# Both layer norms' normalisation moved from VectorE to ScalarE, and a small copy written as a reduction

## What is computed

```python
x = x + attn(layernorm(x))      # 16 heads of 8, causal softmax, w_qkv, w_proj, biases
x = x + ffn(layernorm(x))
# layernorm(x) = (x - mean(x)) / sqrt(var(x) + 1e-5), over the 128 channels, no gain or bias
# ffn: probs = sigmoid(x @ Wg + bg); weights = probs * (probs > 0.5)
#      sum over 8 experts e of weights[:, e] * (relu(x @ W1[e] + b1[e]) @ W2[e] + b2[e]), hidden 512
```

## Time and profile before

| | before |
|---|---|
| median of three runs | 685.77 us (685.29 to 686.74) |
| profiled execution: its own time | 686.17 us |
| its span, first to last instruction | 684.4 us |
| TensorE matmul busy | 650.2 us (95%) |
| VectorE, ScalarE, GpSimd busy | 480.8, 418.6, 330.9 us |
| mean granted TensorE clock | 0.989 of full speed |

### The profile page before, as it was taken

How to read it: one execution, slowest core, us unless ns; L and a number is a source line. 1 busy time by engine, 2 the same in 40 slices (tenths; PEclk the granted TensorE clock), 3 DMA queues, 4 the chain that set the end, 5 groups by cost and what they waited for, 6 DMA issues and landing times.

```text
span 684.4 us, 13158 instructions
## 1 busy us (share of the span) xinstructions
PE 650.2 (95%) x4486; PEld 449.4 (66%) x4486; DVE 480.8 (70%) x958; ACT 418.6 (61%) x793; POOL 330.9 (48%) x409
## 2 busy tenths in 40 slices
PE   2799999999999989999999989999999999999996
PEld 2355666667666766667666756667666766677774
DVE  5797687679876796669866696668866676546443
ACT  2158656667666666676666566666666666665553
POOL 4018434556435454556335555455245564545554
PEclk9799999999999999999999999999999999999998
DMA  6442213210322113210222113220222102100310
GB/s 191 111 125 52 51 42 104 57 42 17 87 73 57 41 26 108 69 42 18 86 63 54 40 39 106 57 56 3 59 87 57 42 2 80 48 17 6 103 32 16
DMA packets 29954, 40.44 MB, mean 59 GB/s; under 512 B 4064, under 2 KB 14184, under 8 KB 29888
## 3 DMA queue, kind: packets, MB, share of 16 engines
q1 hardware_dynamic: 29360, 39.40, 21.4%
q10 hardware_dynamic: 528, 0.20, 0.1%
HBM read 23.72 MB, written 2.23 MB: 38 GB/s over the span
## 4 chain that ended last, share of the span: by engine, by line
PE 85%; DVE 6%; issue 3%; DMA 2%; SPq 2%; POOL 1%; ACT 1%; POOLq 0%; DVEq 0%
PE ring L1166 11%; PE ring L1248 10%; PE ring L1107 9%; PE ring L1109 9%; PE ring L1108 9%; PE y_bank L1293 8%; PE y_bank L1297 8%; PE y_bank L1295 8%; PE ring L1178 6%; PE ring L1113 3%; DVE xn L910 2%; PE ring L1193 2%; DVE negmax L1018 1%; DMA g_w<-in_L_ffn_b 1%; PE ring L1228 1%
## 5 line engine op out<-in xcount | busy, mean ns | idle before, releaser
L863 ACT ACTIVATE h_hi<-ring 128x512 fp32r<-128x512 f32 x256 | 153.4, 599 | 126.2 <-PE ring L1109 110.2
L831 ACT ACTIVATE pt<-ring 128x512 f32<-128x512 f32 x313 | 172.0, 596 | 54.7 <-PE ring L1166 51.8
L762 POOL TENSOR_TENSOR h_lo<-h_all,h_hi 128x512 fp32r<-128x512 f32 x96 | 123.9, 1290 | 149.5 <-ACT h_all L869 149.0
L1018 DVE TENSOR_REDUCE negmax<-ring 128x1 f32<-128x512 f32 (+1 forms) x185 | 119.2, 683 | 74.3 <-PE ring L1178 74.2
L1070 DVE SCALAR_TENSOR_TENSOR h_lo<-ring,h_hi 128x512 fp32r<-128x512 f32 x160 | 109.5, 686 | 56.0 <-ACT h_hi L863 52.7
L755 POOL TENSOR_SCALAR_AFFINE_SELECT pt<-pt 128x512 f32<-128x512 f32 x128 | 80.1, 640 | 110.9 <-ACT pt L831 110.8
L1293 PE MATMUL y_bank<-h_hi,w_lo 128*128 128x512 f32 x256 | 109.0, 426 | 1.1 <-DVE f_buf L1083 0.5
L1107 PE MATMUL ring<-x2T_lo,w_hi 128*128 128x512 f32 x256 | 108.0, 422 | 0.3 <-DVE negmax L1018 0.3
L1166 PE MATMUL ring<-stack 32*128 32x256 f32 (+3 forms) x992 | 94.9, 363 | 8.7 <-DMA stack<-stack 4.8
L1297 PE MATMUL y_bank<-h_lo,w_hi 128*128 128x512 f32 x256 | 100.6, 393 | 0.0
L1109 PE MATMUL ring<-x2T_hi,w_hi 128*128 128x512 f32 x256 | 100.5, 393 | 0.0
(11 more groups left out here) (119 smaller groups left out, 754.1 us busy)
## 6 DMA issues: line engine op xcount, KB each, us to landing
f_buf<-gates SPq DMA_DIRECT2D x64, 256.0 KB, 3.3
stack<-parts SPq DMA_DIRECT2D x96, 128.0 KB
x_in<-in_L_attn_x SPq DMA_DIRECT2D x8, 256.0 KB, 2.9
f_buf<-in_L_ffn_W SPq DMA_DIRECT2D x1, 2048.0 KB, 10.4
out_x<-f_buf SPq DMA_DIRECT2D x8, 256.0 KB, 2.3
stack<-nmT SPq DMA_DIRECT2D x64, 8.0 KB
stack<-stack SPq DMA_DIRECT2D x32, 16.0 KB
bv<-in_L_attn_b_qkv SPq DMA_DIRECT2D x1, 256.0 KB
```

Of the source, the lines that this page charges most:

```text
L762: g_.tensor_tensor(h_lo[:, (i * SLOTS + s) % 3, :], h_all[:], h_hi[:, (i * SLOTS + s) % 3, :].bitcast(F32), ALU.subtract).then_inc(s_hlo_p ...
L831: sc.activation(pt[:, slot, :], b[:], ACT.Exp, scale=SCALE).then_inc(free_sem("ex", i, g, u), 1)
L863: sc.activation(h_hi[:, (i * SLOTS + s) % 3, :], bank_of("z", i, s)[:], ACT.Relu).then_inc(s_hhi, 1)
L1018: v.tensor_reduce(dst, src, AX.X, ALU.max, negate=True).then_inc(free_sem("max", i, g, u), 1)
```

## The change

In `work_items` the items ln1n and ln2n go from VectorE to ScalarE (booked at 1130 instead of 1110 ns), rs1 and rs2 are booked at 1620 instead of 1300, and the waits that follow from it are added. Since the order of all engines comes out of `list_schedule`, it is computed anew. GpSimd now also computes shift = -mean * rstd, and ScalarE computes xn = rstd * x + shift by an activation with a per-partition scale and bias. In `merge` the copy becomes a minimum over one element.

```diff
-         ('dve', 'ln2n', False): 8.5,
+         ('act', 'ln2n', False): 8.5,
...
-            put("sp", ("xload", i), t0 - 30, 600, ("dve", ("ln1n", i - 2)), ("pool", ("xbp", i - 2)))
+            put("sp", ("xload", i), t0 - 30, 600, ("act", ("ln1n", i - 2)), ("pool", ("xbp", i - 2)))
...
-        put("dve", ("ln1b", i), t0 - 20.9, 350, ("dve", ("ln1a", i)))
-        put("pool", ("rs1", i), t0 - 20.8, 1300, ("dve", ("ln1b", i)), ("pool", ("ident", None)))
-        put("dve", ("ln1n", i), t0 - 19, 1110, ("pool", ("rs1", i)), ("pe", ("xT", i - 1)),
+        put("dve", ("ln1b", i), t0 - 20.9, 350, ("dve", ("ln1a", i)), ("pool", ("rs1", i - 1)))
+        put("pool", ("rs1", i), t0 - 20.8, 1620, ("dve", ("ln1b", i)), ("act", ("ln1n", i - 1)), ("pool", ("ident", None)))
+        put("act", ("ln1n", i), t0 - 19, 1130, ("pool", ("rs1", i)), ("pe", ("xT", i - 1)),
             ("pe", ("x2T", i - 3)))
-        put("pe", ("xT", i), t0 - 17, 450, ("dve", ("ln1n", i)), ("pe", ("v", i - 1)))
+        put("pe", ("xT", i), t0 - 17, 450, ("act", ("ln1n", i)), ("pe", ("v", i - 1)))
...
         put("dve", ("proj", i), at + 1.8, 700, ("pe", ("proj", i)), ("pool", ("xbp", i)),
-            ("dve", ("yT", i - 2)))
+            ("dve", ("yT", i - 2)), ("act", ("ln2n", i - 2)))
         put("dve", ("ln2a", i), at + 1.9, 860, ("dve", ("proj", i)))
-        put("dve", ("ln2b", i), at + 1.9, 350, ("dve", ("ln2a", i)))
-        put("pool", ("rs2", i), at + 1.9, 1300, ("dve", ("ln2b", i)))
-        put("dve", ("ln2n", i), at + 2, 1110, ("pool", ("rs2", i)),
+        put("dve", ("ln2b", i), at + 1.9, 350, ("dve", ("ln2a", i)), ("pool", ("rs2", i - 1)))
+        put("pool", ("rs2", i), at + 1.9, 1620, ("dve", ("ln2b", i)), ("act", ("ln2n", i - 1)))
+        put("act", ("ln2n", i), at + 2, 1130, ("pool", ("rs2", i)),
             ("pe", ("xT", min(i + 2, BATCH - 1))), ("pe", ("x2T", i - 1)))
...
                 elif kind in ("rs1", "rs2"):
                     n = int(kind == "rs2")
                     pool.wait_ge(s_aggr[n], (i + 1) * TB)
+                    if i:
+                        pool.wait_ge(s_x2n if n else s_xn, i * TB)
                     g_.tensor_scalar(var[:, n], mv[:, n, :, 1], EPS, None,
                                      ALU.add).then_inc(s_var[n], 1)
-                    pool.wait_ge(s_var[n], i + 1)
-                    g_.tensor_tensor(rstd[:, n], var[:, n], mhalf[:], ALU.pow).then_inc(s_rs[n], 1)
+                    g_.tensor_scalar(shift[:, n], mv[:, n, :, 0], -1.0, None,
+                                     ALU.mult).then_inc(s_var[n], 1)
+                    pool.wait_ge(s_var[n], 3 * i + 2)
+                    g_.tensor_tensor(rstd[:, n], var[:, n], mhalf[:], ALU.pow).then_inc(s_var[n], 1)
+                    pool.wait_ge(s_var[n], 3 * i + 3)
+                    g_.tensor_tensor(shift[:, n], shift[:, n], rstd[:, n],
+                                     ALU.mult).then_inc(s_rs[n], 1)
...
+            def normalise(n, i, src, dst, done):
+                act.wait_ge(s_rs[n], i + 1)
+                for t in range(TB):
+                    sc.activation(dst[:, t, :], src[:, t, :], ACT.Identity,
+                                  bias=shift[:, n, t:t + 1],
+                                  scale=rstd[:, n, t:t + 1]).then_inc(done, 1)
...
+                elif kind == "ln2n":
+                    act.wait_ge(*full("xT", min(i + 2, BATCH - 1)))
+                    if i:
+                        act.wait_ge(*full("x2T", i - 1))
+                    normalise(1, i, x1[:, i % 2], x2n, s_x2n)
...
                     dve.wait_ge(s_stats[n], (i + 1) * TB)
+                    wait(dve, s_rs[n], i)
...
-                else:
-                    dve.wait_ge(s_rs[n], i + 1)
-                    done = s_x2n if n else s_xn
-                    for t in range(TB):
-                        v.tensor_scalar(dst[:, t, :], src[:, t, :], mv[:, n, t, 0:1],
-                                        rstd[:, n, t:t + 1], ALU.subtract,
-                                        ALU.mult).then_inc(done, 1)
...
-                    v.tensor_copy(negmax[:, g, 0], pm[:, :, :, 3]).then_inc(s_merge, 1)
+                    v.tensor_reduce(negmax[:, g, 0], pm[:, :, :, 3:4], AX.X,
+                                    ALU.min).then_inc(s_merge, 1)
...
                     dve.wait_ge(s_xbp, i + 1)
+                    if i >= 2:
+                        dve.wait_ge(s_x2n, (i - 1) * TB)
```

More of the change, by code:

```diff
@@ L174, in work_items @@
         put("dve", ("v", i), t0 + 12.1, 700, ("pe", ("v", i)), ("dve", ("vset", None)))
-        put("pool", ("xbp", i), t0 + 22, 1280, ("dve", ("ln1n", i)), ("dve", ("proj", i - 1)))
+        put("pool", ("xbp", i), t0 + 22, 1280, ("act", ("ln1n", i)), ("dve", ("proj", i - 1)))
         for g in range(GROUPS):
@@ L212, in work_items @@
         put("dve", ("proj", i), at + 1.8, 700, ("pe", ("proj", i)), ("pool", ("xbp", i)),
-            ("dve", ("yT", i - 2)))
+            ("dve", ("yT", i - 2)), ("act", ("ln2n", i - 2)))
         put("dve", ("ln2a", i), at + 1.9, 860, ("dve", ("proj", i)))
-        put("dve", ("ln2b", i), at + 1.9, 350, ("dve", ("ln2a", i)))
-        put("pool", ("rs2", i), at + 1.9, 1300, ("dve", ("ln2b", i)))
-        put("dve", ("ln2n", i), at + 2, 1110, ("pool", ("rs2", i)),
+        put("dve", ("ln2b", i), at + 1.9, 350, ("dve", ("ln2a", i)), ("pool", ("rs2", i - 1)))
+        put("pool", ("rs2", i), at + 1.9, 1620, ("dve", ("ln2b", i)), ("act", ("ln2n", i - 1)))
+        put("act", ("ln2n", i), at + 2, 1130, ("pool", ("rs2", i)),
             ("pe", ("xT", min(i + 2, BATCH - 1))), ("pe", ("x2T", i - 1)))
-        put("pe", ("x2T", i), at + 2.1, 450, ("dve", ("ln2n", i)))
+        put("pe", ("x2T", i), at + 2.1, 450, ("act", ("ln2n", i)))
         put("act", ("x2T", i), at + 2.2, 600, ("pe", ("x2T", i)), ("pe", ("z", i - 2, SLOTS - 1)))
@@ L483, in block_program @@
         rstd = sb("rstd", [P, 2, TB])
+        shift = sb("shift", [P, 2, TB])
         xT = sb("xT", [P, T])
@@ L793, in _ @@
                                   ACT.Copy).then_inc(s_w2hi, 1)
+                elif kind == "ln1n":
+                    if i:
+                        act.wait_ge(*full("xT", i - 1))
+                    if i >= 3:
+                        act.wait_ge(*full("x2T", i - 3))
+                    normalise(0, i, x_in[:, i % 2], xn, s_xn)
+                elif kind == "ln2n":
+                    act.wait_ge(*full("xT", min(i + 2, BATCH - 1)))
+                    if i:
+                        act.wait_ge(*full("x2T", i - 1))
+                    normalise(1, i, x1[:, i % 2], x2n, s_x2n)
                 elif kind == "xT":
@@ L896, in prepare_small_weights, with statistics @@
                 v.memset(wg_lo[:].bitcast(F32), 0.0).then_inc(s_wset, 1)
-            def normalise(n, i, src, dst, step):
+            def statistics(n, i, src, step):
                 if step == "a":
@@ L958, in _ @@
                         dve.wait_ge(s_x[i % 2], 16 * (i // 2 + 1))
[L959 to L963, removed]
+                    statistics(0, i, x_in[:, i % 2], kind[3])
                 elif kind[:3] == "ln2":
@@ L966, in _ @@
                         dve.wait_ge(*emptied("proj", i))
[L967 to L970, removed]
-                    normalise(1, i, x1[:, i % 2], x2n, kind[3])
+                    statistics(1, i, x1[:, i % 2], kind[3])
                 elif kind == "xT":
```

2 lines of the change are left out of this document (1 added, 1 removed).

## The result

| | before | after |
|---|---|---|
| median of five runs each | 685.51 us (685.18 to 686.74) | 688.69 us (688.36 to 689.98) |
| ratio | | 1.0049 [1.0038, 1.006] |
| profiled execution: its own time, its span | 686.17, 684.4 us | 689.98, 688.3 us |

The account below looks back on a forecast made before the run. TensorE, busy 650.2 of 684.4 us, was taken as the bound, so only its holes could be won. Terms -4.1 - 1.0 + 0.4 + 0.4 = -4.3 us gave 681.5 us from a 685.77 median; 8-in-10 range 678.4 to 686.0.

Parts of the forecast that it names:

- The bound and the holes: TensorE bounds the kernel; time off VectorE wins nothing by itself, only TensorE's 7.6 us of waits (168 to 560 us) can.
- Part 2: Normalisation on ScalarE: 455 ns per ACTIVATE, 1.49 us a group; of 5.5 us waits for `xn`, overrun returns 1.4: 4.1 won.
- Part 3: TensorE's "issue" and `parts` waits, 2.1 us: VectorE, freed, is ready earlier; 1.0 us won, bounds 2.1 won and 1.6 lost.
- Part 4: GpSimd's two extra small instructions delay each group 0.5 us, uncovered only at the start: 0.4 us lost, bounds 0 and 0.7.
- Parts 5 to 7: ScalarE's queue behind the groups costs 0.4 us; the added waits cost nothing; the copy as a reduction is worth 0.
- Part 5: Work queued behind groups on ScalarE, tightest `h_all` to GpSimd's `h_lo` with 0.50 us slack: 0.4 us lost, bounds 0 and 1.5.
- A: Rival, chance 0.17: ln2 group comes behind ScalarE's xT copies, so the 1.29 us hole stays and grows by 0.3; 685.5 us.
- B: Rival, chance 0.14: groups delay `h_all`, so TensorE waits 1.0 us for `h_lo`, two groups in each of six sequences; 690.6 us.
- C: Rival, chance 0.03: ScalarE has to load its tables twice, a load taking 1.28 us; 682.8 us.

Follow-up runs that it names:

- e3: The kernel before with only the copy in `merge` written as a one-element reduction: 685.38 us (685.28 before), ratio 0.9992.
- e12: e4 with `shift` allotted last, ln2 groups moved behind the xT copies and ln1 groups behind the `parts` of q: 688.21 us (685.34 before), ratio 1.0043.
- e4: The whole move, but planned in the old order, with the normalisation groups put into ScalarE's list at their old planned times: 694.01 us (685.28 before), ratio 1.0127.
- e9: The changed kernel with attention products (pv) kept out of `y_bank` and `shift` allotted as the last tile: 679.77 us (685.34 before), ratio 0.9921.
- e11: e9 with the copy of merged maxima put back as `tensor_copy`: 679.93 us (685.34 before), ratio 0.9929.
- e1: The changed kernel, its planner keeping attention products (pv) out of `y_bank` while a ring bank is free: 684.20 us (685.28 before), ratio 0.9988.
- e5: The changed kernel with the tile `shift` made 64 instead of 32 bytes per partition: 685.96 us (685.70 before), ratio 1.0009.
- e6: The changed kernel with `shift` of 64 bytes and attention products kept out of `y_bank`: 681.66 us (685.70 before), ratio 0.9942.
- e2: The kernel before with its planner made to put pv(1,0), and with it pv(1,1), into `y_bank`: 690.34 us (685.28 before), ratio 1.007.
- e7: The kernel before with an unused tile of 32 bytes per partition behind `rstd`: 689.58 us (685.70 before), ratio 1.0055.
- e8: The kernel before with an unused tile of 64 bytes per partition behind `rstd`: 686.82 us, ratio 1.0019.
- e14: The kernel before with an unused tile of 96 bytes per partition behind `rstd`: 688.93 us (685.23 before), ratio 1.0056.
- e13: The kernel before with an unused tile of 128 bytes per partition behind `rstd`: 688.24 us (685.23 before), ratio 1.0045.

## Why the prediction was wrong, point by point

**The bound and the holes: right.** TensorE alone counts: VectorE became 30 us lighter, and e3 shows that time off VectorE is worth nothing.

**Part 2, the group on ScalarE: duration nearly right, effect undersized.** The new ACTIVATE, by its line in after, and GpSimd's last small instruction:

```profile
L796 ACT ACTIVATE xn<-x,shift,rstd x32: 476/479/495, 97.3 to 622.5; 128x128 f32<-128x128 f32 x32
L723 POOL TENSOR_TENSOR shift<-shift,rstd x16: 200/200/202, 8.9 to 621.1; 128x4 f32<-128x4 f32 x16
```

479 ns against my 455, a group 1.63 us against 1.49. The Trainium skill's "ScalarE: Activation LUTs", section "What ACT_TABLE_LOAD costs", gives 186 + 2 x 93 + 0.833 x 128 = 479 ns and 1.64 us for a group; the trace agrees on both. But the overrun, 0.5 us now, gives no 1.4 back: the 5.5 us are all won, because the new order puts other matmuls between the transposes (e12, in the old order, keeps 7.2 us of holes). I had argued with the slack of the old order about the new one.

**Part 3, the second kind of hole: right in mechanism, all 2.1 won where I counted 1.0.** The group stands behind `parts`; e4 shows the other place, where the hole grows by 0.3 (I had said 0.4).

**Part 4, the start: undersized.** Timeline of after, against the earlier trace rows:

```profile
8.89 0.20 POOL L723 TENSOR_TENSOR shift<-shift,rstd 128x4 f32<-128x4 f32 x1
9.13 1.65 ACT L796 ACTIVATE xn<-x_in,shift,rstd 128x128 f32<-128x128 f32 x4 [1.09 <-POOL shift L723]
10.92 1.09 PE L1129 MATMUL ring<-ident,xn 128*128 128x128 f32 x4 [10.92 <-ACT xn L796]
```

0.6 us instead of 0.4 up to the first transposes. By the first y e9 is 1.8 us behind before (106.55 against 104.71); where the other 1.2 arise was not followed, and each of the two is one trace's. The end has a piece that I had no term for: the last ln2 group has no cover either. After, and behind it before:

```profile
621.37 1.65 ACT L796 ACTIVATE xn<-x,shift,rstd 128x128 f32<-128x128 f32 x4 [0.47 <-POOL shift L723]
623.16 0.63 PE L1129 MATMUL ring<-ident,xn 128*128 128x128 f32 x4 [0.80 <-ACT xn L796]
```

```profile
620.02 0.61 PE L1113 MATMUL ring<-ident,xn 128*128 128x128 f32 x4
```

In before these transposes start without idle time; in after they wait 0.80 us, in e9 0.92.

**Parts 5 to 7: right.** Part 5 had 0.4 us; in e9 `y_bank` waits for GpSimd's `h_lo` three times, 0.6 us in all, and none of it lies between 168 and 560 us. None of the added waits stands in TensorE's list, and the copy is worth 0 (e3, e11).

**The move alone:** -7.6 for the holes, +1.8 at the start, +0.8 at the end: -5.0 by the rows, -5.6 by e9's median; the two profiled spans differ by 6.4 (684.4 and 678.0), so that the rows don't hold all of it. My -4.3 was near partly by luck: the holes were undersized by 2.5 us (4.1 + 1.0 against 7.6) and the start and end by 2.2 (0.4 against 1.8 + 0.8), and the two errors cancel.

**The step that failed is the sum itself.** It held a term for each instruction moved and each wait added, and none for two things that the diff changes without a line on them. The first is the newly computed order: I read it as the old order with a group in another list, while the planner also gives out banks and dummies anew. It takes the free bank that has been used least; all eight were free at pv(1,0), and that was `y_bank` in after (15 uses, the others 17 to 20) and a ring bank in before (15 uses, `y_bank` 19). This cost 4.5 us (e1; 4.3 from e5 to e6; 5.1 in e2). The second is the addresses behind a new tile of 32 bytes: 2.7 us from after to e5, 4.4 from e1 to e9, 3.9 for the pad alone (e7). The chain from before over e9 and e1 to after, -5.6 + 4.4 + 4.5 = +3.3, must give the measured +3.2 and tests nothing. The test is with the two costs as measured in the kernel before, where nothing was moved: -5.6 + 5.1 (e2) + 3.9 (e7) = +3.4 against +3.2.

**The rivals.** A is shown in e12, and its hole was priced well, though the group took 1.63 us and not 1.49. Its time was 688.2 and not 685.5. A's sum had 0.4 us for the start and nothing for the end; e12 is 0.8 us behind before at the first y (105.52), 1.7 behind at the transposes of 245.58 (247.28) and 2.5 behind at the last ones (622.54 against 620.02), which wait 0.94 us for the group. In the kernel after, its order on ScalarE stands there and its hole doesn't. B did not happen, although the time ended near it: a number that fits is no evidence for its mechanism, and its mark, a wait for `h_lo` in each sequence, is missing. C did not happen either: one table load, as before. The rule in the Trainium skill's "ScalarE: Activation LUTs", section "Rules for kernel authors", to use VectorE and not ScalarE for additions and multiplications, rests there on VectorE's time per element. The trace points the same way, 338 ns in the median for one block on VectorE and 479 on ScalarE. As advice the rule does not hold for this kernel: e9 moves them to ScalarE and is 0.8% faster, ScalarE having the time. That VectorE's collision with GpSimd was what made the old holes is argued from the rows; it was not tested by itself.

## What to carry to other kernels

Where a program computes its order, an edit of costs or engines replaces the whole order; compare banks, first uses and dummies at the start and the end, and the planned end itself (here 4.8 us later in after than in before), before you put a result down to the edit. A new tile goes behind all others, or an unused tile of the same size goes into the kernel before as a control. And when a change does on its own ground what it should and the total still rises, look for the stretch that lost, not for a flaw in the idea.

## What was not expected of the hardware

- **Where tiles start in SBUF changes the pace of matmuls.** An unused tile of 32 bytes costs 0.55% (e7), of 64 bytes 0.19% (e8), of 96 0.56% (e14), of 128 0.45% (e13), with unchanged instructions; from 168 to 560 us and in the last stretch compared above the granted clock is 1.00 in all of them.
- **An idle stretch costs twice.** After 9 us with 5.70 us of work the clock was at 0.61 for the next 4.4 us, and 32 matmuls took 4.06 instead of 2.36 us (e2: 0.62 and 3.73 us; e1, with 7.60 us of work in the 9: 1.00).
- **The long durations belong to the operation, not to the engine.** The same small tile as a copy takes up to 1060 or 960 ns (e11), as a reduction at most 151 (e3). The Trainium skill's "SBUF — State Buffer", section "Who interferes with whom", has this: a copy may take the port pair that VectorE and GpSimd share, a reduction never does. That it came to nothing here is TensorE's doing: none of its waits hung on it.
